# Attention scores in a decoder block: from three bf16 parts over 96 rows to two fp32r parts in two 64-row halves of the array

## What is computed

```python
q = _lin(_lin(x, wq_w, wq_b), vq_w, vq_b)
k = _lin(_lin(x, wk_w, wk_b), vk_w, vk_b)
v = _lin(_lin(x, wv_w, wv_b), vv_w, vv_b)
q = q.reshape(b, s, hc, H).transpose(2, 0, 1, 3)   # 32 heads of 16 columns
scores = jnp.einsum('cbqh,cbkh->cbqk', q, k) / scale
attn = jax.nn.softmax(scores, axis=-1)
o = jnp.einsum('cbqk,cbkh->cbqh', attn, v)
```

## Time and profile before

| | |
|---|---|
| median of 3 runs | 2508.66 us (2508.25 to 2509.22) |
| span of the profiled execution | 2508.5 us |
| TensorE busy | 2341.1 us, 93% of the span |
| VectorE busy | 1798.0 us, 72% |
| ScalarE busy | 1449.9 us, 58% |
| GpSimd busy | 481.4 us, 19% |
| mean granted clock of TensorE | 0.962 |

### The profile page before, as it was taken

How to read it: one execution, slowest core, us unless ns; L and a number is a source line. 1 busy time by engine, 2 the same in 40 slices (tenths; PEclk the granted TensorE clock), 3 DMA queues, 4 the chain that set the end, 5 groups by cost and what they waited for, 6 DMA issues and landing times. The chain is left out here.

```text
span 2508.5 us, 44687 instructions
## 1 busy us (share of the span) xinstructions
PE 2341.1 (93%) x11674; PEld 1167.0 (47%) x11688; DVE 1798.0 (72%) x1934; ACT 1449.9 (58%) x2534; POOL 481.4 (19%) x1070
## 2 busy tenths in 40 slices
PE   8999979999999999999999999999983898888896
PEld 4688843333333333333333333333322786666674
DVE  3577678888888888888888888888823565757665
ACT  0111105777777777777777777777772444444443
POOL 0000000000000000000000000000002566566664
PEclk9999977999999999999999999999996998999898
DMA  3243331112111211211211121121105554535341
GB/s 138 88 126 121 117 87 30 40 37 44 40 38 42 44 35 40 45 39 37 45 40 38 42 43 35 41 45 38 38 7 163 179 176 131 181 102 170 119 137 47
DMA packets 177291, 188.55 MB, mean 75 GB/s; under 512 B 81360, under 2 KB 106960, under 8 KB 177232
## 3 DMA queue, kind: packets, MB, share of 16 engines
q1 hardware_dynamic: 177232, 187.86, 26.8%
HBM read 143.95 MB, written 42.99 MB: 75 GB/s over the span
## 5 line engine op out<-in xcount | busy, mean ns | idle before, releaser
L493 DVE TENSOR_REDUCE neg_max<-psum 128x1 f32<-128x1024 f32 x1024 | 1206.4, 1220 | 276.5 <-PE psum L386 275.8
L474 ACT ACTIVATE probs<-psum 128x512 f32<-128x512 f32 x2048 | 1111.3, 595 | 391.0 <-PE psum L434 389.4
L434 PE MATMUL psum<-q_op,k_op 99*128 99x512 bf16 x2048 | 648.8, 386 | 14.9 <-ACT probs L474 11.0
L386 PE MATMUL psum<-k_op,q_op 96*128 96x512 bf16 x2048 | 546.5, 388 | 15.3 <-DVE k_op L489 11.0
L403 PE MATMUL psum<-probs,v_op 128*32 128x512 f32 x4096 | 544.5, 605 | 1.0 <-ACT probs L474 1.0
L434 PEld LDWEIGHTS psum<-q_op,k_op 99*128 99x128 bf16 x2048 | 158.6, 97 | 670.7 <-ACT probs L474 614.5
L386 PEld LDWEIGHTS psum<-k_op,q_op 96*128 96x128 bf16 x2048 | 291.0, 144 | 209.8 <-DVE neg_max L493 31.4
L528 POOL CAST neg_max_parts<-neg_max 128x8 bf16<-128x8 f32 x128 | 24.2, 189 | 1305.2 <-DVE neg_max L493 1305.2
L146 PE MATMUL psum<-x_hi,conv_w_hi 128*128 128x512 f32 x512 | 209.3, 409 | 6.5 <-DVE x_lo L1153 6.5
L146 PE MATMUL psum<-x_lo,conv_w_hi 128*128 128x512 f32 x512 | 204.4, 399 | 0.0
L146 PE MATMUL psum<-x_hi,conv_w_lo 128*128 128x512 f32 x512 | 204.3, 399 | 0.0
(11 more groups left out here) (100 smaller groups left out, 1895.8 us busy)
## 6 DMA issues: line engine op xcount, KB each, us to landing
conv_w_raw<-in_conv_w_dram SPq DMA_DIRECT2D x64, 512.0 KB, 3.3
qk_parts_dram<-qk_parts SPq DMA_DIRECT2D x64, 384.0 KB, 3.2
q_op<-qk_parts_dram SPq DMA_DIRECT2D x768, 32.0 KB
gate_in<-in_ctx_dram SPq DMA_DIRECT2D x64, 256.0 KB, 3.6
k_op<-qk_parts_dram SPq DMA_DIRECT2D x128, 96.0 KB
x_block<-in_x_t_dram SPq DMA_DIRECT2D x8, 1024.0 KB, 6.2
k_op<-qk_parts_dram SPq DMA_DIRECT2D x128, 64.0 KB
attended_dram<-out SPq DMA_DIRECT2D x256, 32.0 KB
```

What stands on the lines that cost most here:

```text
L386: mm = nc.tensor.matmul(s1_bank[t % 2][:, h * HALF:(h + 1) * HALF], qop[i][0:ROWS, b, t:S:QT], kop[i][0:ROWS, b, h * HALF:(h + 1) * HALF], ...
L434: mm = nc.tensor.matmul(s2_bank[j % 2][:], kop[lo][:, b, kt * P:(kt + 1) * P], qop[lo][:, b, qp * HALF:(qp + 1) * HALF], start=True, stop= ...
L474: nc.scalar.activation(probs[kt % 2][:, j, :], s2_bank[j % 2][:], ACT.Exp, scale=SCALE).then_inc(exp_done, 1)
L493: nc.vector.tensor_reduce(mx[b][:, t:t + 1], s1_bank[t % 2][:], AX_X, ALU.max, negate=True).then_inc(maxed, 1)
```

## The change

q and k are kept in two fp32r parts and no longer in three bf16 parts (a high part, which ACT rounds when it writes it, and a rest, which DVE makes with one instruction from PSUM). A score is then three products of 16 rows, 48 rows, and 50 rows with the two parts of the maximum. The operands are held twice, in rows 0 to 63 and in rows 64 to 127 of the array ("lanes"). The first lane holds the first 512 keys of a batch, the second lane the other 512; the queries are in both.

In attend the order of TensorE becomes, for each step: s2 tiles 0 and 1, one in each lane; one unit of s1, one half of the keys in each lane; s2 tiles 2 and 3, one in each lane; the second unit of s1; pv of the step before. s2 has three banks in place of two (a tile waits for the exponential three before it), pv has one bank in place of two, and there are four `probs` in place of two. The copy of pv's sum is moved to after the second exponential of step 1, and TensorE waits for it (`pv_out`) before the first pv of the slot, in step 1. The last pv of a turn of the loop is now done in the first step of the next turn, and the first turn is written out. A slot's operands are loaded by 10 DMAs for two batches (9 for each batch before), a maximum's parts by 4 (3 before). `k_op` is filled with ones whole before it is loaded.

The same change in project has four buffers of parts in place of two, each 512 KB for a group. The diff, cut:

```diff
-PARTS = 3
-
-
-ROWS = 6 * DH
+PARTS = 2
+
+
+ROWS = 3 * DH
 ROWS_SHIFT = ROWS + PARTS
+LANE = 64
...
-                        n = j % 2
-                        dve.wait_ge(qk_full, (it * 2 + i) * (2 * KC) + j + 9)
-
-                        dve.wait_ge(stored[n], ((it * 2 + i) * KC + j // 2 + 1) * DMA)
-                        s0 = ((it * 2 + i) * (2 * KC) + j) * 3
-                        nc.vector.tensor_copy(parts[n][:, 0, :], full[n][:]).then_inc(step, 1)
-                        dve.wait_ge(step, s0 + 1)
-                        nc.vector.tensor_tensor(rest[n][:], full[n][:], parts[n][:, 0, :],
-                                                ALU.subtract).then_inc(step, 1)
-                        dve.wait_ge(step, s0 + 2)
-                        nc.vector.tensor_copy(parts[n][:, 1, :], rest[n][:]).then_inc(step, 1)
-                        dve.wait_ge(step, s0 + 3)
-                        nc.vector.tensor_tensor(parts[n][:, 2, :], rest[n][:], parts[n][:, 1, :],
-                                                ALU.subtract).then_inc(full_free, 1)
+                        dve.wait_ge(qk_hi, (it * 2 + i) * (2 * KC) + j + 1)
+                        nc.vector.scalar_tensor_tensor(
+                            out=parts[j % 4][:, 1, :], in0=bank[j % 6], scalar=qk_bias[:, j // KC, j % KC:j % KC + 1],
+                            in1=parts[j % 4][:, 0, :].bitcast(F32), op0=ALU.add, op1=ALU.subtract).then_inc(qk_lo, 1)
                     for j in range(2 * KC, GROUPS):
                         dve.wait_ge(proj, (it * 2 + i) * GROUPS + j + 1)
                         nc.vector.tensor_tensor(
...
+    RING = 3
+    DEEP = 4
     with ExitStack() as ctx:
         sb = lambda name, shape, dt: ctx.enter_context(nc.sbuf_tensor(name, shape, dt))
         sem = lambda name: ctx.enter_context(nc.semaphore(name))
-        qop = [sb(f"q_op{i}", [ROWS_SHIFT, B, S], BF16) for i in range(2)]
-        kop = [sb(f"k_op{i}", [ROWS_SHIFT, B, S], BF16) for i in range(2)]
+        qop = [sb(f"q_op{i}", [P, B, S], F32R) for i in range(2)]
+        kop = [sb(f"k_op{i}", [P, B, HALF], F32R) for i in range(2)]
         vop = [sb(f"v_op{i}", [P, B * QT, VW], F32) for i in range(2)]
-        probs = [sb(f"probs{i}", [P, TILES, HALF], F32) for i in range(2)]
+        probs = [sb(f"probs{i}", [P, TILES, HALF], F32) for i in range(DEEP)]
         u = [sb(f"out{i}", [P, HALF], F32) for i in range(2)]
         mx = [sb(f"neg_max{b}", [P, QT], F32) for b in range(B)]
-        mrest = [sb(f"neg_max_rest{b}", [P, QT], F32) for b in range(B)]
-        mparts = [[sb(f"neg_max_parts{i}{b}", [P, PARTS, QT], BF16) for b in range(B)] for i in range(2)]
+        mparts = [[sb(f"neg_max_parts{i}{b}", [P, PARTS, QT], F32R) for b in range(B)] for i in range(2)]
...
-        s2_bank = [bank[4], bank[5]]
-        pv_bank = [bank[6], bank[7]]
-
-        op_in = [[sem(f"op_in{i}{b}") for b in range(B)] for i in range(2)]
...
+            for lane in range(2):
+                r0 = LANE * lane
+                sp.dma_start(qop[i][r0:r0 + 2 * DH, bs, :].bitcast(F32),
+                             qk_scr[0, 0:1, rows, cols].broadcast_to([2, DH, 2 * S])).then_inc(s, DMA)
+                sp.dma_start(qop[i][r0 + 2 * DH:r0 + 3 * DH, bs, :].bitcast(F32), qk_scr[0, 1, rows, cols]).then_inc(s, DMA)
+                for r, part in enumerate((0, 1, 0)):
+                    k = qk_scr[1, part, rows, cols].rearrange("r (b l n) -> r b l n", b=2, l=2)[:, :, lane, :]
+                    sp.dma_start(kop[i][r0 + r * DH:r0 + (r + 1) * DH, bs, :].bitcast(F32), k).then_inc(s, DMA)
+        OPS = 10 * DMA
...
+                def s1_lane(i, b, t, lane):
+                    r = slice(LANE * lane, LANE * lane + ROWS)
+                    return nc.tensor.matmul(s1_bank[t % 2][:, lane * HALF:(lane + 1) * HALF],
+                                            qop[i][r, b, t:S:QT], kop[i][r, b, :], start=True, stop=True)
...
+                def s2(lo, beta, n, j, cell, ready):
+                    lane = (n + j) % 2
+                    r = slice(LANE * lane, LANE * lane + ROWS_SHIFT)
+                    b = 2 * beta + j // 2
+
+                    pe.wait_ge(exp_done, ready)
+                    nc.tensor.matmul(s2_bank[cell % RING], kop[lo][r, b, n // 2 * P:(n // 2 + 1) * P],
+                                     qop[lo][r, b, j % 2 * HALF:(j % 2 + 1) * HALF],
+                                     start=True, stop=True).then_inc(s2_full, 1)
+
+                def pv(s, k, n):
+
+                    pe.wait_ge(exp_done, s * (STEPS * TILES) + n * TILES + TILES + RING)
+                    for j in range(TILES):
+                        kt = n // 2 + QT // 2 * ((n + j) % 2)
+                        mm = nc.tensor.matmul(pv_bank[32 * j:32 * j + 32, :],
+                                              vop[k // 2][:, (2 * (k % 2) + j // 2) * QT + kt, :],
+                                              probs[n % DEEP][:, j, :], start=(n == 0), stop=(n == STEPS - 1))
                     mm.then_inc(pv_step, 1)
 
-                def pv_before(s, k, kt):
-
-                    if kt > 0:
-                        pv(s * STEPS + (kt - 1), k, kt - 1)
-                    elif k > 0:
-                        pv(s * STEPS - 1, k - 1, STEPS - 1)
-
-                def slot(cp, k, more):
+                def slot(cp, k, first, more):
                     lo, beta = k // 2, k % 2
                     s = cp * 4 + k
                     for bl in range(2):
-                        b = 2 * beta + bl
-                        pe.wait_ge(max_in[lo][b], (cp + 1) * MAXES + DMA)
-                        if more or lo == 0:
-                            pe.wait_ge(op_in[1 - lo][b], (cp + 1 + lo) * OPS)
-                    for kt in range(STEPS):
-                        for j in range(TILES):
-                            bl, qp = j // 2, j % 2
-                            b = 2 * beta + bl
-                            if j == 2 and (more or lo == 0):
-                                for n in (kt * 2, kt * 2 + 1):
-                                    s1_unit(1 - lo, 2 * beta + n // QT, n % QT, s * 16 + n + 32)
-                            elif j == 2:
-                                pv_before(s, k, kt)
-
-                            pe.wait_ge(exp_done, s * (4 * STEPS) + kt * 4 + j + 1)
-                            mm = nc.tensor.matmul(s2_bank[j % 2][:], kop[lo][:, b, kt * P:(kt + 1) * P],
-                                                  qop[lo][:, b, qp * HALF:(qp + 1) * HALF], start=True, stop=True)
-                            mm.then_inc(s2_full, 1)
-                        if more or lo == 0:
-                            pv_before(s, k, kt)
-                        if kt == 0:
+                        pe.wait_ge(max_in[lo][2 * beta + bl], (cp + 1) * MAXES + DMA)
+                    if more or lo == 0:
+                        pe.wait_ge(op_in[1 - lo][beta], (cp + 1 + lo) * OPS)
+                    for n in range(STEPS):
+                        for half in range(2):
+                            unit = 2 * n + half
+                            for side in range(2):
+                                j = 2 * half + side
+                                cell = k * (STEPS * TILES) + n * TILES + j
+                                ready = s * (STEPS * TILES) + n * TILES + j + (2 if cell < 2 else 1)
+                                s2(lo, beta, n, j, cell, ready)
+                            if more or lo == 0:
+                                b, t = 2 * beta + unit // QT, unit % QT
+                                pe.wait_ge(maxed, s * 16 + unit + 31)
+                                s1_lane(1 - lo, b, t, n % 2)
+                                s1_lane(1 - lo, b, t, (n + 1) % 2).then_inc(s1_full, 1)
+                        if n == 1:
                             if beta == 0:
                                 pe.wait_ge(v_ready, cp * 2 + lo + 1)
 
                             pe.wait_ge(pv_out, s + 1)
-                    if k == 3:
-                        pv(s * STEPS + (STEPS - 1), k, STEPS - 1)
-
-                with pe.Fori(0, LAST) as cp:
+                        if n > 0:
+                            pv(s, k, n - 1)
+                        elif not (first and k == 0):
+                            pv(s - 1, (k - 1) % 4, STEPS - 1)
...
+                for k in range(4):
+                    slot(0, k, True, True)
+                with pe.Fori(1, LAST) as cp:
                     for k in range(4):
-                        slot(cp, k, True)
+                        slot(cp, k, False, True)
                 for k in range(4):
-                    slot(LAST, k, False)
+                    slot(LAST, k, False, False)
+                pv(LAST * 4 + 3, 3, STEPS - 1)
...
+                def evacuate(s, k, uses):
+
+                    act.wait_ge(pv_step, s * STEPS + STEPS + DEEP)
+                    act.wait_ge(u_stored[k % 2], uses * U_STORE + DMA)
```

(64 more changed lines are left out.)

96 lines of the change are left out of this document (45 added, 51 removed).

## The result

| | before | after |
|---|---|---|
| median of 4 runs each | 2508.9 us | 2582.5 us (2572.6 to 2590.9) |
| span of the profiled execution | 2508.5 us | 2577.1 us |
| mean granted clock of TensorE | 0.962 | 0.925 |
| one turn of the loop, from the third on | 93.0 us | 92.4 us |

The ratio is 1.028 with a 95% interval of 1.025 to 1.031: the changed kernel is 2.8% slower, where 0.6% faster was forecast. A turn of the loop is as fast as forecast. The time is lost before and around the loop's steady part.

A forecast was written before the change was run, and what follows sets the result against it. A step was taken as bound by the chain through the first exponential, not by matmul work. From 2508.7 us, -22 + 19.5 + 1.1 - 10 - 4.4 + 1 = -15 gave 2493 us, range 2440 to 2600.

The forecast's parts named there:

- The sign: Whole kernel: 15 us less time; chances faster 0.51, same 0.11, slower 0.38.
- the chain: Attention step: first exponential, fourth s2 tile, s1's second lane, pv, next step in a row; chance 0.57.
- The step: Attention loop at full clock: 2.84 us a step against 2.88, 22 us less over 496 steps.
- Full overlap of the lanes: Score matmuls in the two row halves run together, assumed without a trace row; step 2.84 us.
- missing overlap: Rival, score matmuls: lanes do not run together, step 3.07 us, +85, 2593 us; chance 0.15.
- blocked loads: Rival, s1's second lane: load waits for the same lane's matmul, step 2.95, 2540 us; chance 0.16.
- The free loads: Rival, fp32r loads in lanes: uncovered loads cost nothing, step 2.62, 2387 us; chance 0.10.
- The single pv bank: Attention slots: pv waits for the copy, 0.32 us in one step of each slot, +19.5 us over 61 slots.
- The turn's end: End of each loop turn: no pv drained before the branch any more, 10 us less, bounds 0 and 11.
- The last two slots: Slots without s1: step 2.61 us against 2.89, 4.4 us less.
- The start: Start of attend: fill of `k_op` and larger loads against faster first maxima, net +1 us, bounds -2 and +5.
- The clock: TensorE's granted clock: added idle time need not lower it; a falling clock with anything else, chance 0.02.

The follow-up runs named there:

- d_copy_early: Changed kernel with the copy of pv's sum behind the first exponential of step 1 instead of the second: 2572.3 us.
- h_one_lane: Changed kernel with every s1 and s2 matmul in the first lane, so none overlap, same amount of work: 3862.8 us.
- n_before_66_rows: Kernel before, without lanes, s1 and s2 matmuls over 66 rows instead of 96 and 99, exponential's scale made small: 3403.3 us.
- k_fill_step: Changed kernel plus one unused bf16 matmul over 128 rows, 256 columns, in every step: 2517.3 us.
- l_combo: Changed kernel plus the extra matmul per step, the earlier copy of pv's sum and SP's altered start order: 2493.4 us, 0.993 of the kernel before.
- m_pv_first_fill: Changed kernel with pv ahead of the fourth s2 tile, an extra full-height matmul per step and SP's altered start order: 2583 to 3556 us.
- e_pv_first: Changed kernel with pv of the step before ahead of the fourth s2 tile, copy of pv's sum moved to step 0: 2535.9 us.

## Why the prediction was wrong

The sign was wrong; the chain was right. That 2582.5 lies in the stated range of 2440 to 2600 is luck: its upper end was drawn for lanes that do not overlap (2593), and they did overlap.

- **The step.** Forecast 2.84 at full clock, measured 2.85. The release of the fourth tile was forecast at 1.18 and came at 1.19. Full overlap of the lanes was taken without a row for it and is shown. The two rivals that priced missing overlap or blocked loads are out at this clock: two loads for the two lanes start together, and s1's loads at 1006.04 start while the matmuls of s2 still run in the same lanes. The free loads are out as well: the first matmul still takes 0.50.
- **The single pv bank.** Forecast 0.32 a slot, measured 0.30 (3.15 against 2.85), and `d_copy_early` removed it.
- **The turn's end.** No loss there after the change, as taken; a whole turn was 92.4 against 93.0, where the forecast's own terms give 32 x 2.84 + 4 x 0.32 = 92.2.
- **The last two slots.** 2.61 forecast, 2.60 measured as long as the clock was 1.00. It fell at 1923 us, and the last five steps took 4.07.
- **The start.** This term was mis-sized: +1 us with bounds of -2 and +5, measured +18. The first operands had landed only at 369, not about 358, with TensorE waiting on them, and the first slot then waited 7 us for the parts of the maxima. I had counted issues on SP's queue and the fill, and given the transfers no price, though they had no cover here: the argument that each load has a whole slot of time holds inside the loop only. The pace of the maxima gave 2 us back, as forecast. In the kernel before, TensorE's first wait had ended with the fill of `k_op` by VectorE, not with a transfer; with the fill out of the way the transfers set the start. That wait, and the two of the changed kernel:

```profile
355.36 1.93 PE L386 MATMUL psum<-k_op,q_op 96*128 96x512 bf16 x4 [11.02 <-DVE k_op L489]
```

```profile
369.12 1.25 PE L372 MATMUL psum<-k_op,q_op 48*128 48x512 f32 x4 [25.61 <-DMA k_op<-qk_parts_dram]
...
411.36 0.32 PEld L391 LDWEIGHTS psum<-q_op,k_op 50*128 50x128 f32 x2 [6.99 <-DMA q_op<-neg_max_parts]
```

- **The clock.** This is the step that failed. The prediction said that the idle time which the change brings need not bring down the clock, and rested on a stretch with idle time at 1.00. But the matmuls of that stretch used 99 rows. The change lowers the rows of a matmul to 48 and 50, and `h_one_lane` (48 and 50 rows) shows that the clock can then stay at 0.50 with no idle time at all; `n_before_66_rows` points the same way, with its reserves. I gave a falling clock 0.02 together with everything else. Spans of 15 us less were forecast and 69 more measured, 84 apart. About 60 of these are the clock's (some 51 in the first two turns: 143.5 + 95.4 less twice 92.4, less the 3 that the kernel before lost there too; 8 or 9 in the last slots), and 17 the start's. The start's miss alone would have used up the forecast gain, so the clock explains the size of the loss and not the sign alone: with it nearly held, `k_fill_step` came to 2517, no better than the kernel before, and only `l_combo`, with the two avoidable waits gone as well, to 2493.

What stays open: what ends a half-clock stretch once it has begun (218, 239, 273 and 287 us in four near-identical kernels), why `m_pv_first_fill` never left it in the profiled run, and whether it is the rows as such, or something that goes with them, that the clock follows. The scatter of the changed kernel's runs, 2572.6 to 2590.9, would be explained by it; that was not traced run by run.

## What to carry to other kernels

Halving TensorE's work gains only what lies on the chain that sets the step; find the chain first, and see whether the matmuls were not already hidden beside it. When a change takes rows or columns of the array out of use, look at the granted clock of every stretch, above all behind a pause, and give the risk a price: a few cheap matmuls over the whole array in a gap can be worth more than the work that was saved, as in `k_fill_step`. They are no sure cure, as `m_pv_first_fill` shows, so read the clock again after each change of order. Transfers at the start of a stage have none of the cover that the same transfers have inside its loop.

## What the runs showed of the hardware

- Two fp32r matmuls in the two 64-row halves ran fully in parallel, loads included: 0.50 us for both, where one takes 0.50.
- The granted clock stayed at 0.50 for 2758 us with TensorE busy in all of them, when every score matmul used 48 or 50 rows; the same kernel with both halves in use rose to 1.00 after 153 us, and one 128-row matmul of 256 columns in each step brought this to 12 us (`k_fill_step`), while in another order the clock stayed at 0.50 with it (`m_pv_first_fill`).
- Once at 1.00 the changed kernel's order held it for over 1300 us with TensorE busy for 92% of the time, while the order with a step of 2.61 lost it again and again, with TensorE busy for 1389.5 of 1444 us (`e_pv_first`).
